# A four-layer image kernel on one core: in layer 0, recurrence scores by head on 32 rows each, two abreast; the layer norm inside the recurrence; the causal filter in twelve steps

## The reference, cut to what matters

```python
x1: h = layernorm(seq, ln_w, ln_b)                      # over the 192 channels of a token
    x_in, z = split(h @ w_up + b_up, 2)                 # 2 x 384
    x_conv = sum(x_pad[:, t:t+s] * conv_k[:, t]) + conv_b   # causal filter, 4 steps
    x_act = silu(x_conv);  q = x_act @ w_q;  k = x_act @ w_k;  v = x_in
    i_pre, f_pre = [q, k, v] @ w_i + b_i, [q, k, v] @ w_f + b_f
    hs = mlstm_scan(q, k / sqrt(32), v, i_pre, f_pre)   # 12 heads of 32, a gated recurrence over tokens
    hn = (hs - mean) / sqrt(var + 1e-5) * mh_w + mh_b   # per head
    seq + ((hn + skip * x_act) * silu(z)) @ w_down + b_down
y = x1 + silu(seq @ w_lin + b_lin)
y = conv3x3(y) + conv2_b;  batch norm over the images;  leaky relu
```

## Time and profile before

| | us |
|---|---|
| time, median of 3 runs (lowest to highest) | 9894.38 (9889.97 to 9896.47) |
| the profiled execution: its time | 9886.75 |
| the profiled execution: span from first to last instruction | 9885.1 |
| busy over the span: TensorE, VectorE, ScalarE, GpSimd | 7440.3, 6338.2, 3833.8, 1975.7 |
| layer 0 | about the first 3740 |

### The profile page before, as it was taken

How to read it: one execution, slowest core, us unless ns; L and a number is a source line. 1 busy time by engine, 2 the same in 40 slices (tenths; PEclk the granted TensorE clock), 3 DMA queues, 4 the chain that set the end, 5 groups by cost and what they waited for, 6 DMA issues and landing times.

```text
span 9885.1 us, 90874 instructions
## 1 busy us (share of the span) xinstructions
PE 7440.3 (75%) x31150; PEld 2987.0 (30%) x31150; DVE 6338.2 (64%) x11557; ACT 3833.8 (39%) x7464; POOL 1975.7 (20%) x1768
## 2 busy tenths in 40 slices
PE   7989998999999985657677667667767766866743
PEld 4444444444444441112222222222222221222211
DVE  5555555555555553376876876777687687687645
ACT  3333333333333332443453354354344335435411
POOL 0000000000000000031442342243144134234223
PEclk9999999999999997668778778878877877887866
DMA  0000000000000001033454444345345444444444
GB/s 32 7 7 10 7 7 7 7 7 7 7 7 7 7 7 68 13 107 104 132 155 111 123 140 128 107 141 146 97 140 151 109 129 145 122 108 140 138 126 132
DMA packets 292848, 777.33 MB, mean 79 GB/s; under 512 B 59302, under 2 KB 125938, under 8 KB 292004
## 3 DMA queue, kind: packets, MB, share of 16 engines
q0 software_dynamic: 92160, 453.06, 14.5%
q1 hardware_dynamic: 198916, 316.40, 12.6%
q10 hardware_dynamic: 1312, 2.07, 0.1%
HBM read 514.22 MB, written 96.49 MB: 62 GB/s over the span
## 4 chain that ended last, share of the span: by engine, by line
PE 45%; DVE 24%; SPq 7%; ACT 7%; DMA 7%; issue 5%; POOL 4%; DVEq 0%; ACTq 0%; POOLq 0%
DVE arena L2194 6%; SPq L2540 5%; PE ps L924 4%; PE ps L2505 4%; DVE arena L1771 4%; PE ps L1007 3%; DMA arena<-img,arena 3%; PE ps L970 3%; PE ps L1244 3%; PE ps L2516 2%; PE ps L2061 2%; SPq L2356 2%; PE ps L702 2%; PE ps L2486 2%; POOL arena L2318 2%
## 5 line engine op out<-in xcount | busy, mean ns | idle before, releaser
L2194 DVE SCALAR_TENSOR_TENSOR arena<-arena 128x192 f32<-128x192 f32 x3456 | 1627.1, 488 | 321.9 <-ACT arena L2236 239.4
L2318 POOL DMA_INDIRECT arena<-img,arena x1152 | 1273.1, 1105 | 2648.0 <-DMA img<-arena 1960.6
L2505 PE MATMUL ps<-arena 128*64 128x512 f32 x3072 | 873.0, 689 | 242.8 <-DMA arena<-arena 241.9
L1771 DVE TENSOR_REDUCE arena<-ps 128x2 f32<-128x1024 f32 x768 | 892.4, 1217 | 250.8 <-PE ps L2040 245.0
L2061 PE MATMUL ps<-arena 128*64 128x512 f32 x3072 | 949.6, 716 | 2.2 <-ACT arena L1915 2.1
L1915 ACT ACTIVATE arena<-ps 128x512 f32<-128x512 f32 x1536 | 819.1, 600 | 179.4 <-PE ps L2071 176.7
L944 POOL MEMSET arena<- 76x1024 bf16 x16 | 15.4, 960 | 3444.0 <-PE ps L970 3444.0
L1052 DVE TENSOR_TENSOR arena<-ps,arena 128x512 f32<-128x512 f32 x384 | 265.5, 691 | 678.3 <-PE ps L1007 602.9
L2236 ACT ACTIVATE arena<-arena 128x192 f32<-128x192 f32 x1152 | 502.1, 457 | 504.6 <-DMA arena<-img,arena 501.1
L1083 ACT ACTIVATE arena<-ps,arena 128x128 f32<-128x128 f32 x1536 | 439.1, 368 | 649.0 <-PE ps L1002 648.8
L2071 PE MATMUL ps<-arena 32*128 32x512 bf16 x1536 | 378.8, 452 | 314.1 <-ACT arena L1922 205.3
(11 more groups left out here) (340 smaller groups left out, 12141.9 us busy)
## 6 DMA issues: line engine op xcount, KB each, us to landing
arena<-arena SPq DMA_DIRECT2D x2048, 76.5 KB, 2.1
img<-arena SPq DMA_DIRECT2D x256, 192.0 KB, 4.1
arena<-y SPq DMA_DIRECT2D x32, 768.0 KB, 5.6
arena<-img,arena POOLq DMA_INDIRECT x1152, 4.5
arena<-x SPq DMA_DIRECT2D x32, 384.0 KB, 6.5
y<-arena SPq DMA_DIRECT2D x32, 384.0 KB, 3.0
out<-arena SPq DMA_DIRECT2D x16, 768.0 KB, 4.3
arena<-x SPq DMA_DIRECT2D x16, 512.0 KB, 3.8
```

Of the source, the lines that this page charges most:

```text
L1771: dve.tensor_reduce(out, self.wides[B.at("max", b, g, n, h) // 2].rearrange("p (a b) -> p a b", a=2), AX.X, AL.max).then_inc(*S.mark("max_ ...
L2194: i = dve.scalar_tensor_tensor(tk[:, k, :], gb[:, 192 * q:192 * q + 192], self.w4[:, q, n:n + 1], tk[:, k, :], AL.mult, AL.add)
L2318: pool.indirect_dma_start(self.g[n % 6], None, img, bass.IndirectOffsetOnAxis(ap=ii[:, n:n + 1], axis=0)).then_inc(*S.landed(f"gather{n % ...
L2505: i = pe.matmul(ps[64 * t:64 * t + 64, :], self.dg[J % 2][:, o:o + 2, :].rearrange("p a b -> p (a b)"), win, start=n == 0, stop=n == 2)
```

## The change

Everything lies in layer 0.

- Scores: no block-diagonal `qd`. For each n four fp32 matmuls of 32 rows and 128 columns straight from kk and qq, heads 0 and 1 between L999 and the decay matmuls, heads 2 and 3 after them. Heads 0, 2 go to one bank and 1, 3 to another, each held for a pair of n; a matmul waits on TensorE's own semaphore for the one before in its bank. VectorE multiplies once per pair, in two instructions of 512 columns. `back` comes two n later in place of one; `acc` holds one bank in place of two.
- The layer norm (`pe_layer`, `dve_layer`, `act_layer`) is moved from `enter` to `ahead`, so it stands inside `chunks` behind n = 16 to 19. `h0` gets memory of its own, and `yo` shares with `lnr`.
- The filter (`dve_filter`) is twelve steps: one and three of them in VectorE's norm, 2, 2 and 4 behind the three y sums of `join`; it writes the memory of dx and px.
- Gates: the transposes for "a" and "k" stand one n earlier (n = 2 and 3), the splits too (n = 3 and 4).
- Six taps of `conv(b-1)` run before `scan(b)`, twelve are woven in. The skip scaling moves into `chunks` (n = 2, 4, 6). The DMA of y is issued in two parts.

```diff
@@ pe_chunks
+        po, acc_free = B.hold(("acc", b), ("o_act", b, 7))
+        def scores(banks, n, heads):
+            c, g = divmod(n, 3)
+            sl = slice(128 * c, 128 * c + 128)
+            for j in heads:
+                r, o = slice(32 * j, 32 * j + 32), 256 * (n % 2) + 128 * (j // 2)
+                if j > 1:
+                    pe.wait_ge(*S("s_pe", b, n, j - 2))
+                elif n % 2:
+                    pe.wait_ge(*S("s_pe", b, n - 1, j + 2))
+                pe.matmul(banks[j % 2][:, o:o + 128], kk[r, g, sl], qq[r, g, sl], start=True, stop=True).then_inc(*S.mark("s_pe", b, n, j))
...
+            px, v1, kt = self.px[n // 2 % 2][:, n % 2], self.v1[c % 2], self.kt[c % 2]
             if g == 0:
+                if c:
+                    pe.wait_ge(*S("o_act", b, c - 1))
...
+            pe.wait_ge(*S("p_dve", b, n // 2))
...
+        for n in range(24):
+            if g == 0:      # transposes of k and v, as before
...
+            if n % 2 == 0:
+                banks = []
+                for q in range(2):
+                    ps, free = B.hold(("s", b, n // 2, q), ("p_dve", b, n // 2))
+                    pe.wait_ge(*free)
+                    banks.append(ps)
+            pd, free = B.take(("pd", b, n), ("d_act", b, n))
             pe.wait_ge(*free)
+            pe.wait_ge(*S("gate_act", b, "last", 0))
+            pe.matmul(pd[:, :], self.idb, self.mkb, start=True, stop=False)
+            scores(banks, n, (0, 1))
+            for j in range(4):
+                h = 4 * g + j
+                i = pe.matmul(pd[:, 128 * j:128 * j + 128], self.esb[:, 32 * h:32 * h + 1].to_broadcast([76, 128]), self.gs[0][:, sl], start=False, stop=j == 3)
+            i.then_inc(*S.mark("d_pe", b, n))
+            scores(banks, n, (2, 3))
+            if n % 2:
+                for q in range(2):
+                    B.drop(("s", b, n // 2, q))
+            if n > 1:
+                back(n - 2)
+            yield
+        for n in (22, 23):
+            back(n)
+            yield
@@ dve_chunks
-            for j in range(4):
-                i = dve.tensor_copy(qd[32 * j:32 * j + 32, j, :], qq[32 * j:32 * j + 32, g, sl])
+            if g == 0:      # keys scaled, as before
+            if n % 2:
+                m = n // 2
+                dx, px = self.dx[m % 2], self.px[m % 2]
                 dve.wait_ge(*S("d_act", b, n))
+                dve.wait_ge(*S("pv_pe", b, n - 4))
+                for q in range(2):
+                    dve.wait_ge(*S("s_pe", b, n, 2 + q))
+                    i = dve.tensor_tensor(px[:, :, q::2, :], B("s", b, m, q)[:, :].rearrange("p (n j t) -> p n j t", n=2, j=2), dx[:, :, q::2, :], AL.mult)
+                i.then_inc(*S.mark("p_dve", b, m))
+            if n in (2, 4, 6):      # skip scaling of block n // 2 - 1
+            if n > 1:
+                back(n - 2)
@@ ahead
         yield from self.gn.dve(dve, b, xn, [(f"x_in{b % 2}", b, 2), ("prep0", "all")])
+        yield from self.dve_layer(dve, b)
...
+        yield from self.pe_layer(pe, b)
...
+        yield from self.act_layer(act, b)
@@ dve_filter
+        dve.wait_ge(*S("pv_pe", b - 1, 23))
         for m in range(3):
+            dst, src = self.fl[m], self.xin[:, m, :]
             dve.wait_ge(*S("up_act", b, m, 1))
             dve.tensor_scalar(dst, src[:, 0:1024], W["CK"][:, m, 0:1], W["CB"][:, m:m + 1], AL.mult, AL.add).then_inc(*S.mark("filter", b, m, 0))
+            yield
             for j in range(1, 4):
                 dve.wait_ge(*S("filter", b, m, j - 1))
                 dve.scalar_tensor_tensor(dst, src[:, j:j + 1024], W["CK"][:, m, j:j + 1], dst, AL.mult, AL.add).then_inc(*S.mark("filter", b, m, j))
                 yield
@@ dve_norm, dve_join
+        run(some(self.filter, 1))       # behind the reciprocal
+        run(some(self.filter, 3))       # behind the variance
+            run(some(self.filter, 4 if n == 2 else 2))      # behind each y
@@ act_project (pe_project likewise: n == 3 to 2, n == 4 to 3)
-            if n == 3:
+            if n == 2:
                 act.wait_ge(*S("gate_dve", b, "k"))
...
-            if n > 3:
-                split(n - 4)
+            if n in (3, 4):
+                split(n - 3)
@@ stages
-                weave((scan(b), 33), (conv(b - 1), 18))
+                g = conv(b - 1)
+                run(some(g, 6))
+                weave((scan(b), 35), (g, 12))
...
-                weave((norm(b), 8), (enter(b + 1), 10))
+                weave((norm(b), 8), (enter(b + 1), 6))
```

More of the change, by code:

```diff
@@ L563, in __init__ @@
         at = ar.at
[L564 to L567, removed]
+        self.dx = [ar([128, 2, 4, 128]) for _ in range(2)]
+        self.px = [ar([128, 2, 4, 128]) for _ in range(2)]
+        self.sml = Arena(ar.tile, at)([128, 5, 96])
+        self.fl = [v.rearrange("p a b c -> p (a b c)") for v in (self.dx[1], *self.px)]
         self.kt = [ar([128, 384]) for _ in range(2)]
@@ L779, in dve_project @@
         r8 = lambda v: v.rearrange("p (c n) -> p c n", c=8)
+        if b == 0:
+            run(self.dve_filter(dve, b))
         yield
@@ L800, in dve_project @@
         dve.tensor_tensor(r8(g2), r8(fg), bc(self.mp[:, :], 128), AL.add).then_inc(*S.mark("gate_dve", b, "l"))
-        yield from skip(4)
+        yield from skip(3)
         ps = B("gates_t", b)
@@ L969, in back @@
                 h = 4 * g + j
-                i = pe.matmul(po[:, 33 * h:33 * h + 33], px[:, 128 * j:128 * j + 128], v1[:, 33 * h:33 * h + 33], start=False, stop=j == 3)
+                i = pe.matmul(po[:, 33 * h:33 * h + 33], px[:, j, :], v1[:, 33 * h:33 * h + 33], start=False, stop=j == 3)
             i.then_inc(*S.mark("pv_pe", b, n))
@@ L1011, in pe_chunks @@
-        back(7, 2)
-        for p in range(2):
-            B.drop(("acc", b, p))
+            if g == 0:
+                ps, free = B.take(("kt", b, c), ("kt_dve", b, c))
+                pe.wait_ge(*free)
+                pe.wait_ge(*S("qk_act", b, 5, 1))
+                for m in range(3):
+                    i = pe.transpose(ps[:, 128 * m:128 * m + 128], kk[:, m, sl], C["ID"])
+                i.then_inc(*S.mark("t_pe", b, c, "k"))
+                ps, free = B.take(("v1", b, c), ("v1_act", b, c))
+                pe.wait_ge(*free)
+                for m in range(3):
+                    i = pe.transpose(ps[:, 128 * m:128 * m + 128], xin[:, m, 3 + 128 * c:131 + 128 * c], C["ID"])
+                i.then_inc(*S.mark("t_pe", b, c, "v"))
@@ L1062, in act_chunks, with back @@
+            if n in (2, 4, 6):
+                m = n // 2 - 1
+                dve.tensor_scalar(self.xa[:, m, :], self.xa[:, m, :], W["SK"][:, m:m + 1], W["MB"][:, m:m + 1], AL.mult, AL.add).then_inc(*S.mark("norm_dve", b, "skip", m))
+            if n > 1:
+                back(n - 2)
+            yield
+        for n in (22, 23):
+            back(n)
+            yield
     def act_chunks(self, act, b):
         S, B = self.S, self.B
-        def back(c, g):
+        def back(n):
+            c, g = divmod(n, 3)
@@ L1088, in act_chunks @@
-        back(7, 2)
+            act.activation(self.osb[:, c, :], B("acc", b)[:, 0:396], ACT.Copy).then_inc(*S.mark("o_act", b, c))
+        for n in range(24):
+            c, g = divmod(n, 3)
+            if g == 0:
+                act.wait_ge(*S("t_pe", b, c, "v"))
+                act.wait_ge(*S("u_pe", b, c - 2))
+                act.activation(self.v1[c % 2].rearrange("p (h d) -> p h d", h=12)[:, :, 0:32], B("v1", b, c)[:, 0:384].rearrange("p (h d) -> p h d", h=12), ACT.Copy).then_inc(*S.mark("v1_act", b, c))
+            dx = self.dx[n // 2 % 2]
+            act.wait_ge(*S("d_pe", b, n))
+            act.wait_ge(*S("p_dve", b, n // 2 - 2))
+            act.table(ACT.Exp)
+            for j in range(4):
+                i = act.activation(dx[:, n % 2, j, :], B("pd", b, n)[:, 128 * j:128 * j + 128], ACT.Exp, bias=self.gat[:, c, 4 * g + j:4 * g + j + 1])
+            i.then_inc(*S.mark("d_act", b, n))
+            if n > 1:
+                back(n - 2)
+            yield
@@ L1098, in dve_norm @@
         r_, s_, v_, u_, w_ = (self.sml[:, n, :] for n in range(5))
-        for m in range(3):
-            dve.tensor_scalar(self.xa[:, m, :], self.xa[:, m, :], W["SK"][:, m:m + 1], W["MB"][:, m:m + 1], AL.mult, AL.add).then_inc(*S.mark("norm_dve", b, "skip", m))
+        self.filter = self.dve_filter(dve, b + 1) if b + 1 < self.NB else iter(())
         yield
```

166 lines of the change are left out of this document (52 added, 114 removed).

## The result

The changed kernel takes 10406.6 us (10394.5 to 10421.4 in 4 runs), the kernel before 9893.0 in the runs beside it (9890.0 to 9896.5): 1.052 times as long, 95% interval 1.0501 to 1.0538. I had foreseen 9974 and a range of 9790 to 10090. The sign was right and the size was not, 513 us in place of 80.

What follows compares the result with a forecast made beforehand. TensorE's order of work was taken as the bound. Stages of 24.4, 17.6, 67.7 and 118.1 us plus 8.1 for the clock gave a period of 235.9, 4.8 more; times 15, plus 8, it forecast 9974 us, range 9790 to 10090.

Steps and rivals of the forecast that it cites:

- Entry, join, project: Stages 1 to 3 of a period: 24.4 us (a gain of 19.3), 17.6, and 67.7 (10.4 more).
- Price of a pair: Scores in the recurrence: two 32-row, 128-column matmuls abreast take 0.42 us, load and end included.
- loads pulled ahead: Rival, scores: weight loads run under the matmul before, an n is 1.1 in place of 1.63; 9844 us, chance 0.14.
- pairs not abreast: Rival, scores: the second of a pair starts only after the first, a pair is 0.64; 10088 us, chance 0.12.
- front of an n: Recurrence, TensorE's work ahead of each state product: 1.63 us in place of 1.36, 6.5 us more over 24 n.
- Waits in the recurrence: Recurrence: product and state waits sum to 9.0 us; the layer norm's mean waits 3.4, its waits in all 5.0.
- Sum of the recurrence at full clock: Stage 4: 114.0 us less taps, half clock and old waits, plus scores, new waits and layer norm, gives 118.1.
- The clock: TensorE's clock falls behind two new waits: 4.1 us for the mean and 4.0 for "a" a period; otherwise full clock.
- the clock stays up: Rival: the isolated waits for "a" and the mean don't lower TensorE's clock; 9852 us, chance 0.18.
- all four new waits halve the clock: Rival: the two waits left at full clock, 2.5 and 2.3 us, cost 4 each too; 10090 us, chance 0.08.
- Image 0: First image has no taps to hide the product at n = 6, 12, 18; with the last scan's dearer scores, +8 us.

Runs made afterwards that it cites:

- full_rows: Changed kernel with each score matmul on all 128 rows in place of its head's 32 (result wrong): 9942.2 us, ratio 0.9989 to the kernel before.
- before_few: Kernel before the change with each n's score matmul streaming 128 of its 512 columns (result wrong): 9861.0 us, ratio 0.9963.
- old_scores: Changed kernel with the scores, recurrence and its buffers as before the change, the rest of the change kept: 9845.6 us, ratio 0.9892 to the kernel before.
- bank_choice: Changed kernel, but in the recurrence the next PSUM bank is the one expected free first, not the next in turn: 10408.6 us, ratio 1.0463 to the kernel before.
- changes: full_rows plus one 32-row, 4-column matmul ahead of each score pair, so four shape changes an n: 10468.3 us, ratio 1.0569 to the kernel before.
- no_changes: full_rows plus one 128-row, 4-column matmul ahead of each score pair, so no shape change: 10114.7 us in one run.
- few_columns: Changed kernel with score matmuls of 128 rows but only 32 columns (result wrong): 10158.1 us in one run, beside 9895.9 for the kernel before.
- together: Changed kernel with an n's four score matmuls in one place behind the decay, two shape changes instead of four: 10366.2 us, ratio 1.0474 to the kernel before.
- rows64: Changed kernel with every score matmul on 64 rows in place of 32 (result wrong): 10338.9 us in one run, beside 9895.9 for the kernel before.
- dense1: Changed kernel with one idle full bf16 matmul of 512 columns more in each n: 10576.4 us in one run.
- dense: Changed kernel with three idle full bf16 matmuls of 512 columns more ahead of each n's decay: 10328.6 us, ratio 1.0444 to the kernel before.
- tuned: old_scores with a and k transposes behind their n's matmuls, one tap fewer before the gates, the norm's square a block earlier: 9623.8 us, ratio 0.9722 to the kernel before.

## Why the prediction was right in its sum and wrong in its time

**Entry, join, project**: right. 24.4, 17.6 and 67.7 us were forecast; 24.0 and 24.1, 17.0, and 67.4 and 70.4 came in the two periods that I read, as did their waits ("a" 3.0 forecast and 2.8 measured, gates 2.5 and 2.3).

**Price of a pair**: right at 0.42, from the nearest rows. The rivals "loads pulled ahead" (0.21) and "pairs not abreast" (0.64) both fall with it. The front of an n was right too. From the decay's first matmul to the state product it takes 1.49 in the changed kernel and 1.38 in full_rows, and behind it the state product takes 0.33 and 0.23:

```profile
1206.93 0.39 PE L1030 MATMUL ps<-arena 128*128 128x512 bf16 x1 [0.90 <-DVE arena L1082]
...
1208.42 0.49 PE L990 MATMUL ps<-arena 128*128 128x132 f32 x2
```

```profile
1301.14 0.38 PE L1030 MATMUL ps<-arena 128*128 128x512 bf16 x1
...
1302.52 0.39 PE L990 MATMUL ps<-arena 128*128 128x132 f32 x2
```

Forecast was 1.63 with the state product's load; 1.49 and the 0.10 are 1.59. An n of the changed kernel thus has 0.2 us more than one of full_rows, 5 us an image.

**Waits in the recurrence**: the mean's 3.4 us came to the tenth. Product and state, 9.0 forecast, show 9.1 where the clock stays up (full_rows), which is in part luck: its n is 0.2 shorter and so hides less of each wait. In the changed kernel itself they are 5.0: at 1.2 GHz TensorE takes longer and VectorE doesn't, so half-speed work hides them.

**Sum of the recurrence at full clock**: 118.1 forecast. The changed kernel never showed it. Two estimates lie on either side. full_rows took 118.5 us, of which 3.4 are the two falls behind product and mean; with the 5 us of the longer n that makes 120. The changed kernel's 150.8 less 41 for the clock, with 4 for the waits that half speed hid, makes 114. full_rows' whole period, 228.7 against my 227.8, agrees so well because the 5.1 us of its falls and the 5 us of its shorter n happen to be the same, which is luck.

**The clock**: this is the step that failed. I gave it 8.1 us a period, 4.1 behind the mean and 4.0 behind "a", and left the rest of the recurrence at full clock without a reason. The part on the waits was sound in kind. In full_rows the waits of 3.36 and 2.83 are each followed by 0.50 for 3.4 us, which costs 1.7 and not 4; in the changed kernel the clock is at 0.50 for 6.8 us around the mean's matmul (1277.9 to 1284.7), 3.4 lost, and the stage of "a" takes 67.4 at 1.00 in one period and 70.4 at 0.95 in the next. The wait of 2.3 for the gates, which I had left at full clock, is followed by no fall in full_rows and by 3.4 us at 0.50 in the changed kernel (1185.7 to 1189.1); the product's wait of 2.15, to which I had given nothing either, is followed by one in both. The rival "the clock stays up" thus didn't come about. But all these falls together make only a small part of the 41 us (5.1 a period in full_rows). What was wrong is the term that I put at nothing, the clock in the recurrence's own work. There the fall needs no long wait: the stretches at full clock that go ahead of one above are 5.75 of 6.8 and 9.53 of 10.3 us busy, the second with no wait over 0.4 that the timeline shows, and those at half speed 6.90 of 6.9 and 9.84 of 10.2. I had taken this work for dense because TensorE was busy in it. In place of 8.1 for the whole period the clock took up to 41 us of the 150.8, less the 4 of waits that it hid. My rival "all four new waits halve the clock" looked for it in the waits again and came to 16 us a period; no rival let the recurrence's own work lose the clock. The row that should have warned me was the earlier trace rows: L1007, which the change takes out, is the longest matmul of an n, 0.91 of 1.36 us in front, 512 columns on the full array. Cut to 128 columns it leaves the kernel before at 0.84 (before_few).

**Image 0**: I gave it and the last scan 8 us together. It has no filter taps beside its recurrence. Before, then after:

```profile
144.60:231.70 87.10, 78.96 (x532) 0.97 0.00 1
```

```profile
147.80:299.00 151.20, 140.46 (x671) 0.55 0.00 1
```

And full_rows:

```profile
147.50:256.80 109.30, 93.81 (x684) 0.89 0.00 1
```

64 us more in this one, at a clock of 0.55 where it had 0.97. Without the taps, which are matmuls of 512 columns, the recurrence is at 1.2 GHz for 90% of the time. Scores on all rows bring 42 of the 64 back, so most of it is the same cause; that the missing taps are what makes it stronger here is argued and not shown.

**What is shown and what is open.** Shown: the scores carry the loss (old_scores), and of them the 32-row tiles (full_rows); the waits don't (full_rows, bank_choice); four changes of shape an n cost 0.11 of the clock with the matmuls and their columns the same (changes, and no_changes in one run); fewer columns cost it with no change of shape added (few_columns 0.79 in one run, before_few 0.84). The changed kernel has the changes of shape, and its scores fill less of the array, 32 rows a tile; it stands at 0.73, below the 0.81 of changes. How the two divide its fall isn't settled: together halves the changes and gains 0.02, rows64 doubles the rows and gains 0.02. That dense1 gains nothing and dense 0.14 says that the clock doesn't rise in proportion to work added, and no run tells why. The Trainium skill (TensorE: Matmul & The Clock Gate, "A second HAM failure mode: psum-queue depth-cycling") tells of a kernel whose clock oscillates because TensorE idles very briefly, and often, between groups of matmuls, there with banks of PSUM in turn. The pair changes and no_changes shows such a clock, 0.81 against 0.92 for 48 added pairs of shape changes an image, but not the idle time: by the rows TensorE is busy for 152.52 of 159.3 us in changes and 120.30 of 129.8 in no_changes. Whether the array stands still at a change of shape is thus open.

## What to carry to other kernels

Before full-array matmuls are cut down to small tiles, ask what keeps TensorE's clock up: work that is cheaper by its columns can be dearer in time, as few_columns shows (a quarter of full_rows' score columns, 137.2 us against 118.5), or gain next to nothing, as before_few does (16 us less work, 3 us less time). Put a number on the clock for the whole stage in which the work gets thinner or changes shape often, not only for the gaps around it, and make "the stage runs at 1.2 GHz for half of its time" a rival with its price. Single waits of 2 to 3 us in full-array work come after that: in full_rows each cost itself and 1.7 us of clock behind it. They are still worth taking out once the clock holds, as tuned shows (ratio 0.9722 against 0.9892 of old_scores).

## What the runs showed of the hardware that I had not expected

- The clock falls to 0.50 out of a stretch that is 5.75 of 6.8 us busy, in work whose twin with full-array scores ran at 0.97, and TensorE is busy back to back at half speed (6.90 of 6.9 us).
- Four changes of shape an n, by matmuls of 4 columns, cost 25 us an image over the same matmuls without a change, about 7 by themselves and 18 by the clock.
- Adding work can save time: three useless matmuls in each n took the recurrence from 150.8 to 145.6 us (clock 0.73 to 0.87), while one made it 158.7 (0.72).
- Waits of 2.15, 2.83 and 3.36 us amid full-array work were each followed by one stretch of 3.4 us at 0.50, 1.7 us lost, alike for all three; one of 2.32 (for the gates) by none. The recurrence's mean clock stayed at 0.97.
